# A quantised FFN on one Trainium2 core: new start-up transfers, down scales folded into the weights, two middle operations moved to GpSimd, deeper buffers

## The reference

```python
W = weights[condition]                       # (64, 32, 32), picked by token out of 16
y = einsum('bct,bcd->bdt', x, W)             # x: (64, 32, 512) f32
x_flat = y.reshape(-1, 512).astype(bfloat16) # 2048 rows
def _dynamic_quant(x, inv_smooth):
    xs = x.astype(float32) * inv_smooth
    scale = maximum(max(abs(xs), axis=-1) / 127, 1e-08)
    return clip(round(xs / scale), -127, 127), scale
gate_out = (qg @ w_gate.T) * sg * s_wgate    # 512 -> 256
up_out   = (qu @ w_up.T) * su * s_wup        # 512 -> 256
inter = clip(silu(gate_out) * up_out, -10, 10).astype(bfloat16)
qi, si = _dynamic_quant(inter, inv_inter)
out = x + (qi @ w_down.T) * si * s_wdown     # 256 -> 512
```

## Time and profile before

| | us |
|---|---|
| median of 3 runs | 96.28 |
| lowest and highest run | 96.28, 98.17 |
| span of the profiled execution | 96.0 |
| DVE busy | 72.1 (75%) |
| POOL busy | 67.5 (70%) |
| ACT busy | 62.9 (66%) |
| PE busy | 57.0 (59%) |

### The profile page before, as it was taken

How to read it: one execution, slowest core, us unless ns; L and a number is a source line. 1 busy time by engine, 2 the same in 40 slices (tenths; PEclk the granted TensorE clock), 3 DMA queues, 4 the chain that set the end, 5 groups by cost and what they waited for, 6 DMA issues and landing times.

```text
span 96.0 us, 1583 instructions
## 1 busy us (share of the span) xinstructions
PE 57.0 (59%) x425; PEld 36.1 (38%) x430; DVE 72.1 (75%) x174; ACT 62.9 (66%) x113; POOL 67.5 (70%) x57
## 2 busy tenths in 40 slices
PE   0692737189559487595865958569594574305610
PEld 0691214164426344363443635436352353102100
DVE  5300059407798989999999999999999999996360
ACT  5000226813978999889898898988989878223100
POOL 5505094800858759999999999999999746925720
PEclk9999999966999999999999999999999999965555
DMA  1989639989412312063360633202202022020443
GB/s 33 230 291 376 180 106 272 251 153 321 136 43 73 111 22 92 38 181 117 112 219 6 213 111 111 109 7 109 91 18 109 3 109 106 7 109 0 180 149 114
DMA packets 8796, 12.05 MB, mean 126 GB/s; under 512 B 3026, under 2 KB 3922, under 8 KB 8786
## 3 DMA queue, kind: packets, MB, share of 16 engines
q1 hardware_dynamic: 7906, 10.08, 33.0%
q0 software_dynamic: 400, 1.31, 3.8%
q10 hardware_dynamic: 480, 0.54, 2.7%
HBM read 7.47 MB, written 4.46 MB: 124 GB/s over the span
## 4 chain that ended last, share of the span: by engine, by line
DVE 54%; issue 13%; DMA 11%; PE 11%; ACT 4%; POOL 2%; SPq 1%; POOLq 0%; ACTq 0%
DVE y_ps L359 13%; DVE ffn L406 12%; DVE gu L373 10%; DVE gu_ps L378 7%; DMA raw<-in_L_ffn_w_down 6%; PE gu_ps L582 5%; DMA picked<-in_L_cond_weights,tokens 5%; DVE amax_m L390 4%; PE o_ps L610 3%; ACT q_t L269 3%; DVE rscale L367 2%; PE y_ps L560 2%; POOL raw L195 1%; DVE rest L414 1%; DVE rest_sums L418 1%
## 5 line engine op out<-in xcount | busy, mean ns | idle before, releaser
L206 POOL TENSOR_TENSOR xs<-y_bf,inv_in 128x1024 f32<-128x1024 bf16 x15 | 32.1, 2142 | 10.2 <-ACT y_bf L255 9.6
L582 PE MATMUL gu_ps<-w_t,q_t 128*128 128x256 bf16 x128 | 17.6, 283 | 17.4 <-ACT q_t L269 17.4
L262 ACT ACTIVATE q<-xs,rscale 128x512 f32<-128x512 f32 x32 | 21.4, 724 | 2.1 <-DVE rscale L367 2.1
L222 POOL TENSOR_TENSOR res<-ffn,x_sb 128x512 f32<-128x512 f32 x15 | 19.1, 1271 | 2.7 <-DVE ffn L406 2.7
L359 DVE TENSOR_REDUCE y_ps<-xs 128x2 f32<-128x1024 f32 x16 | 19.5, 1217 | 1.1 <-POOL xs L204 1.1
L560 PE MATMUL y_ps<-x_sb,mix_all 128*128 128x512 f32 x32 | 17.3, 625 | 4.7 <-DMA mix_all<-in_L_cond_weights 2.5
L582 PEld LDWEIGHTS gu_ps<-w_t,q_t 128*128 128x128 bf16 x128 | 11.7, 101 | 21.4 <-ACT q_t L269 20.0
L269 ACT ACTIVATE q_t<-qt_ps 128x1024 bf16<-128x1024 f16 x16 | 16.2, 1014 | 0.3 <-PE qt_ps L566 0.3
L255 ACT ACTIVATE y_bf<-y_ps 128x512 bf16<-128x512 f32 x16 | 9.3, 581 | 10.1 <-PE y_ps L560 10.1
L373 DVE TENSOR_TENSOR gu<-gu_ps,s_in 128x512 f32<-128x512 f32 x16 | 10.9, 683 | 5.5 <-PE gu_ps L582 5.5
L215 POOL TENSOR_TENSOR xm<-clipped,inv_mid 128x256 f32<-128x256 bf16 x16 | 11.7, 732 | 3.6 <-DVE clipped L385 3.6
(11 more groups left out here) (40 smaller groups left out, 54.1 us busy)
## 6 DMA issues: line engine op xcount, KB each, us to landing
x_sb<-in_x SPq DMA_DIRECT2D x16, 256.0 KB, 3.5
out<-res SPq DMA_DIRECT2D x16, 256.0 KB, 2.0
raw<-in_L_ffn_w_gate POOLq DMA_DIRECT2D x1, 512.0 KB
raw<-in_L_ffn_w_up POOLq DMA_DIRECT2D x1, 512.0 KB, 7.6
raw<-in_L_ffn_w_down SPq DMA_DIRECT2D x1, 512.0 KB, 5.6
inv_in<-in_L_ffn_inv_gate ACTq DMA_DIRECT2D x1, 256.0 KB, 4.2
inv_in<-in_L_ffn_inv_up ACTq DMA_DIRECT2D x1, 256.0 KB, 5.5
picked_dram<-picked SPq DMA_DIRECT2D x1, 256.0 KB, 3.2
```

The lines of the kernel that those rows point to most:

```text
L206: nc.gpsimd.tensor_tensor(xs[t % 2][:, :, :], y_bf[t % 2][:, :].unsqueeze(1).to_broadcast([P, 2, T]), inv_in[:, :, :], ALU.mult).then_inc( ...
L222: nc.gpsimd.tensor_tensor(res[t % RES][:, :], ffn[t % 2][:, :], x_sb[:, t * T:(t + 1) * T], ALU.add).then_inc(res_done, 1)
L262: nc.scalar.activation(q[t % 2][:, m, :], xs[t % 2][:, m, :], ACT.Copy, bias=ROUND_TO_F16, scale=rscale[:, t, m:m + 1]).then_inc(q_done, 1)
L582: last = nc.tensor.matmul(gu_ps[p][:, m, :], q_t[p][:, m, c, :], w_t[j][:, m, c * I:(c + 1) * I], start=(j == 0 and c == 0), stop=(j == pa ...
```

## The change

The host now lays the weights out: gate, up and down come already transposed by 128-row chunks, and all six vectors come as one row `vectors`. On the chip:

- **Vectors.** One transfer puts the row on one partition; five PE products with a row of ones (`widen`) spread it over 128 partitions in PSUM, and ACT and DVE copy the parts out. The broadcast transfers go.
- **Weights.** Gate and up products read the top halves of the f32 numbers directly as moving operand (every second bf16); the transposes and copies go. ACT issues their transfers, behind its first copy.
- **Down weights.** DVE multiplies w_down by s_down (`fold_s_down`) and splits the f32 result into three bf16 parts (`next_part`). Each down tile takes six products instead of two. `down_out` multiplies by the row scale and adds x, straight into `res`; POOL's `residual` goes.
- **Register loads.** The tokens for the early blocks are loaded from DRAM, in groups of two or four ahead of the transfers; the SBUF row goes.
- **Middle.** The clip and the middle quantisation are POOL's. The intermediate goes to SBUF as bf16. The scales of tile t+3 and of the middle of tile t are one operation over three columns, from SBUF to SBUF.
- **Buffers.** `xs` four, `y_bf`, `q`, `q_t`, `gu` and the middle's three each; the mix product waits for `ybf_done` and runs five tiles ahead.
- **End tiles.** Tiles 0 and 15 go through smoothing, maximum, quantisation and transposing in halves; tile 15's down product and output are two halves.
- 36 warming products instead of 52. The check of the weights' low bits moves to the start, and covers gate and up only.

```diff
-    WARM_UP = 52
+    WARM_UP = 36
...
+    XS, YB, QB, GB, MB = 4, 3, 3, 3, 3
+    MID_LAG = 3
...
@@ SP
-            sp.dma_start(token_row[:, :], token.unsqueeze(0)).then_inc(row_in, 16)
+            sp.dma_start(rows[:, :], vectors.unsqueeze(0)).then_inc(rows_in, 16)
             load(0)
-            load(1)
-            sp.wait_ge(row_in, 16)
...
+            for t in range(EARLY):
+                s = [sp.value_load(token.unsqueeze(0)[0:1, t * PER + j:t * PER + j + 1], min_val=0, max_val=S - 1)
+                     for j in range(PER if t == 2 else PER // 2)]
+                if t == 0:
+                    sp.wait_ge(mix_zero, 1)
+                for j in range(len(s)):
+                    early_block(t, j, s[j])
+                if t + 1 < EARLY:
+                    load(t + 1)
+            sp.dma_start(flat(raw_down), w_down).then_inc(w_down_in, 16)
+            load(3)
             sp.wait_ge(picked_in, 16)
             sp.dma_start(picked_dram, picked[:, :]).then_inc(picked_out, 16)
...
+            load(4)
             sp.wait_ge(picked_out, 16)
...
@@ POOL
+            def clip(t):
+                pool.wait_ge(inter_done, t + 1)
+                nc.gpsimd.tensor_scalar(clipped[t % MB][:, :], inter[t % MB][:, :], LIMIT, -LIMIT,
+                                        ALU.min, ALU.max).then_inc(clip_done, 1)
...
+            def quantise_mid(t):
+                pool.wait_ge(rscale_done, scales_through(t + MID_LAG, 2))
+                if t >= MB:
+                    pool.wait_ge(qmt_done, t - MB + 1)
+                nc.gpsimd.tensor_scalar(qm[t % MB][:, :], xm[t % MB][:, :], rscale[:, t + MID_LAG, 2:3], ROUND_TO_F16,
+                                        ALU.mult, ALU.add).then_inc(qm_done, 1)
...
+            for t in range(4):
+                smooth(t)
+            for i in range(TILES):
+                clip(i)
+                smooth_mid(i)
+                if exists(i + 4):
+                    smooth(i + 4)
+                quantise_mid(i)
...
@@ ACT
+            inv_gate_copy()
+            act.dma_start(raw[0][:, 0, :], w_gate).then_inc(w_in, 16)
+            act.dma_start(raw[0][:, 1, :], w_up).then_inc(w_in, 16)
+            y_out(0)
+            s_in_copy()
+            y_out(1)
+            y_out(2)
+            quantise(0)
+            y_out(3)
+            q_out(0)
+            quantise(1)
+            y_out(4)
+            for i in range(TILES + 1):
                 if exists(i):
+                    gate_silu(i)
+                if exists(i + 1):
+                    q_out(i + 1)
+                if exists(i + 2):
+                    quantise(i + 2)
+                if exists(i - 1):
+                    qm_out(i - 1)
+                if exists(i + 5):
+                    y_out(i + 5)
...
@@ DVE
+            rest_in_gate_up()
+            fold_s_down()
+            for i in range(TILES + 1):
                 if exists(i):
+                    gate_up_out(i)
+                if exists(i - 1):
+                    amax_mid(i - 1)
+                if i == LAST - 3:
+                    smooth_gate(LAST)
+                if i == LAST - 2:
+                    amax_half(LAST, 1)
+                scales(i + 2)
                 if exists(i):
+                    intermediate(i)
+                if i + 3 < LAST:
+                    amax_in(i + 3)
...
+                if i == 0:
                     raise_flag()
+                    next_part(1)
+                if i == 1:
+                    next_part(2)
+                if exists(i - 2) and i - 2 < LAST:
+                    down_out(i - 2)
+            for h in range(2):
+                down_out_half(h)
...
+                nc.vector.scalar_tensor_tensor(res[t % RES][:, :], o_ps[:, :], scale[:, t + MID_LAG, 2:3],
+                                               x_sb[:, t * T:(t + 1) * T], ALU.mult, ALU.add).then_inc(res_done, 1)
...
@@ PE
+            def widen(dst, at, n):
+
+                return nc.tensor.matmul(dst, ones_row[:, :], rows[:, at:at + n], start=True, stop=True)
...
+                        last = nc.tensor.matmul(gu_ps[p][:, m, :], q_t[a][:, m, c, :],
+                                                bf16_top(raw[j][:, m, c * I:(c + 1) * I]),
+                                                start=(j == 0 and c == 0), stop=(j == parts - 1 and c == TC - 1))
...
+            def down_products(a, dst, first, end):
+                for j in range(PARTS):
                     for c in range(IC):
+                        last = nc.tensor.matmul(dst, qm_t[a][:, c, :],
+                                                bf16_top(w_out[j][:, c, first:end]),
+                                                start=(j == 0 and c == 0), stop=(j == PARTS - 1 and c == IC - 1))
...
+            for t in range(4):
+                mix_in_batch(t)
             transpose_q(0)
+            mix_in_batch(4)
+            for i in range(TILES + 2):
+                if exists(i - 2):
+                    transpose_mid(i - 2)
                 if exists(i):
+                    gate_up(i)
...
+                if exists(i + 1):
+                    transpose_q(i + 1)
                 if exists(i - 2):
+                    down(i - 2)
+                if exists(i + 5):
+                    mix_in_batch(i + 5)
```

More of the change, by code:

```diff
@@ L14, with adaln_ffn @@
 ROUND_TO_F16 = float(3 * 2 ** 22 + OFFSET_BITS)
-def adaln_ffn(nc, x, token, mix_w, w_gate, s_gate, w_up, s_up, w_down, s_down, inv_gate, inv_up, inv_inter, out):
+def adaln_ffn(nc, x, token, mix_w, w_gate, w_up, w_down, vectors, out):
     B, C, T = x.shape
     S = mix_w.shape[0]
-    I = w_gate.shape[0]
     PER = P // C
     TILES = B * C // P
+    LAST = TILES - 1
     PARTS = 3
-    TC, IC = T // P, I // P
+    TC = T // P
+    I = w_gate.shape[1] // TC
+    IC = I // P
     EARLY = 3
-    WARM_UP = 52
+    WARM_UP = 36
     RES = 4
-    AHEAD = 4
+    XS, YB, QB, GB, MB = 4, 3, 3, 3, 3
+    MID_LAG = 3
+    AT_INV, AT_S_IN, AT_MID, AT_OUT = 0, 2 * T, 2 * T + 2 * I, 2 * T + 3 * I
     x_rows = x.rearrange("b c t -> (b c) t")
@@ L175, in _ @@
                              ).then_inc(blocks_in, 16)
-            sp.dma_start(inv_mid[:, :], inv_inter.partition_broadcast(P)).then_inc(mid_in, 16)
-            sp.dma_start(s_out[:, :], s_down.partition_broadcast(P)).then_inc(s_out_in, 16)
-            for t in range(4, 11):
+            for t in range(5, 12):
                 load(t)
-            for t in range(TILES):
+            for t in range(LAST):
                 store(t)
-                if exists(t + 11):
-                    load(t + 11)
+                if exists(t + 12):
+                    load(t + 12)
@@ new lines, in q_out @@
+                if split(t):
+                    for m in range(2):
+                        act.wait_ge(qt_done, 2 * t + 1 + m)
+                        nc.scalar.activation(q_t[t % QB][:, m, :, :], qt_half(t, m), ACT.Copy,
+                                             bias=-float(OFFSET)).then_inc(qt_out, 1)
+                else:
+                    act.wait_ge(qt_done, 2 * t + 2)
+                    nc.scalar.activation(q_t[t % QB][:, :, :, :], qt_ps[t % 2][:, :, :, :], ACT.Copy,
+                                         bias=-float(OFFSET)).then_inc(qt_out, 1)
@@ L420, in raise_flag @@
             def raise_flag():
                 dve.wait_ge(rest_total, 1)
[L422 removed]
+                nc.vector.tensor_copy(flag[:, :], flag_ps).then_inc(flag_done, 1)
             def again(t):
@@ L671, with by_chunks @@
     from concourse.bass_utils import run_bass_kernel_spmd
+    def by_chunks(w):
+        columns, contracted = w.shape
+        return np.ascontiguousarray(w.T.reshape(contracted // P, P, columns).transpose(1, 0, 2).reshape(P, -1))
+    laid_out = {
+        "x": inputs["x"], "token": inputs["itok_B_0_15"], "mix_w": inputs["L0_cond_weights"],
+        "w_gate": by_chunks(inputs["L0_ffn_w_gate"]), "w_up": by_chunks(inputs["L0_ffn_w_up"]),
+        "w_down": by_chunks(inputs["L0_ffn_w_down"]),
+        "vectors": np.concatenate([inputs[n] for n in (
+            "L0_ffn_inv_gate", "L0_ffn_inv_up", "L0_ffn_s_wgate", "L0_ffn_s_wup", "L0_ffn_inv_inter", "L0_ffn_s_wdown")]),
+    }
     nc = bacc.Bacc("TRN2", target_bir_lowering=False, num_devices=1)
     arrays, args = {}, []
-    for name in _INS:
-        a = np.ascontiguousarray(inputs[name])
+    for name, value in laid_out.items():
+        a = np.ascontiguousarray(value)
         arrays[f"in_{name}"] = a
```

563 lines of the change are left out of this document (251 added, 312 removed).

## The result

| | before | after |
|---|---|---|
| median, us | 97.22 | 112.66 |
| lowest and highest, us | 96.28, 99.25 | 112.32, 112.86 |
| span of the profiled execution, us | 96.0 | 110.8 |
| ratio after / before | | 1.1657, 95% interval 1.1593 to 1.172 |

The ratio and its interval go by the fast runs of both kernels alone, so the ratio isn't the quotient of the medians; in experiment 1 they leave out one run of 126.85 us.

A forecast was written before the change was run, and what follows sets the result against it. DVE and POOL together bound the middle, a chain of transfers the head. The terms 20.6 + 5.2 + 8.4 + 38.0 + 9.85 + 11.25 gave a 93.3 us span, with 0.28 added 93.6 us, range 89.5 to 99.0.

The forecast's parts named there:

- L: Head, SP's queue: time to load one register value from DRAM, 0.4 us taken; gather's store starts at 10.4 + 8L.
- Rival C: Head: eight DRAM register loads in series hold SP's queue; at L = 1.3 the time is 100.8 us; chance 17%.
- Landing of the store: Head: the store of the gathered blocks takes 2.8 us to land, against 3.26 in the kernel before.
- From the blocks to the first result: Head: from the landing of the fourth tile's blocks to the first gate/up result, 5.2 us at the low clock.
- The merged scale: Steady turn, DVE: the scale operation over three columns takes 0.15 us.
- rival D: Steady turn: the three-column scale is blocked by POOL's 2.11 us smooth; turn 4.2, time 98 us; chance 10%.
- The turn without the wait: Steady turn, PE and POOL setting the pace: 3.8 us, bounds 3.65 and 4.15; ten turns 38.0.
- Rival E: PE's products: strided moving operands run at half rate; turn 6.0, time 115 us; chance 3%.
- First two turns: DVE's first two turns, with later parts of w_down and the flag: 4.4 and 4.05, together 8.4 us.
- Last three turns: Turns without mix or whole smooth, last tile in halves: 3.65, 3.3 and 2.9, together 9.85 us.
- The tail: From the last gate/up result to the end of the span: 11.25 us, 2.7 of it twelve 256-column products.
- Around the span: Added to the 93.3 us span to get the median of the runs: 0.28 us, giving 93.6.

The follow-up runs named there:

- experiment 1: Changed kernel with its register loads read from SBUF again, after one small transfer of the token row: 101.81 us, ratio to the kernel before 1.0459.
- run 3: Changed kernel with two early tiles instead of three, so SP loads four registers from DRAM instead of eight: 108.12 us in one run.
- experiment 2: Changed kernel with the merged three-column scale cut into three one-column operations: 107.92 us, ratio to the kernel before 1.1149.
- experiment 10: Changed kernel with 52 warming products instead of 36: 112.96 us in one run.
- run 6: Changed kernel with both register loads from SBUF and one-column scale operations: 97.6 us, ratio to the kernel before 1.0055.
- run 4: Kernel before with the input maximum in SBUF instead of PSUM, so its two-column scale goes from SBUF to SBUF: 119.07 us in one run.
- experiment 5: Kernel before with the register loads of its early blocks read from DRAM, nothing else changed: 111.69 us in one run.
- number 8: Kernel of experiment 7 with the check of the low bits moved ahead of the first tile's smoothing: 95.53 us, ratio to the kernel before 0.9845.
- experiment 7: Changed kernel with SBUF register loads, one-column scales and a reordered head (four early blocks, earlier gather store, 52 warming products): 95.99 us, ratio to before 0.9865.

## Why the prediction was wrong, point by point

- **The register load, the step that failed worst.** The sum had L = 0.4 for one load. It argued from one end, "the nearest row is the same instruction by far", and that row read SBUF. What was mis-sized is not the latency alone: a value from DRAM is two loads in series, of which the trace of before could show neither. L, the two loads together, measured 1.60 in the mean, and 10.4 + 8L = 23.2 against 23.59 measured: the rest of that term held. That is 10.0 us of the head's 13.1. Rival C named the place and the mechanism; its L of 1.3 was still too low. "Issued in groups, several may be in flight" was the reason given against it, and no two loads overlap in the trace. The Trainium skill (Runtime: NRT & Kernel Launch, The launch sequence) tells of about 1.3 us for register loads from HBM; measured are 0.92 and 0.46 in the median for the pair, 1.39 together, so this figure was near. The Trainium skill (DMA: Bandwidth & Descriptors, Latency and other measured facts) has a floor of about 600 ns; the single load of 463 ns lies below it, the pair far above, and the measurement decides.
- **Landing of the store.** Forecast 2.8, measured 5.1 in the changed kernel and 7.2 in run 3: +2.3 us. The reason given, that less is in flight, didn't hold: the core moved 256 GB/s in that stretch of the changed kernel and 216 in the kernel before. That traffic is the cause isn't shown: experiments 2 and 10, with the changed kernel's order of transfers, have 4.3 and 4.4 us at 300 GB/s. From the scatters to mix(3) 4.2 was forecast, 4.0 measured.
- **From the blocks to the first result.** 5.2 forecast, 6.3 measured; the low clock was foreseen from the earlier trace rows, but lasted into the gate/up products as well (1.64 for 1.07). In run 6 the same stretch took 5.7.
- **The merged scale.** The forecast's price of 0.15 was wrong; rival D, given 10%, was right: it works the turn out as 4.2, and 4.17 is measured, with each of its parts within 0.1 us of the trace. The reason against it, that a scale of one column took 136 ns, was true, and carried over to three columns where it doesn't hold: 152 ns for one, 746 for three. Runs 2 and 4 show this both ways. The Trainium skill (VectorE: DVE Perf Modes, Mode 2×_2P) says that an operation with one SBUF source and an SBUF destination can read its tensor through both ports, split along its outermost dimension; with what the Trainium skill (SBUF — State Buffer, Who interferes with whom) says of the lock, this fits every scale operation here: two and three columns stand, one column and the two columns from PSUM don't. No run shows the ports themselves, and the reciprocal of three columns from SBUF to SBUF, 0.18 beside a smooth in run 2, shows that size and place of the operands don't settle it.
- **C and D as exclusive cases.** Both were listed with the time that each would give alone, and no case held both. They are independent, both occurred, and their prices add. The case of both, with C's L of 1.3, would have read 100.8 + 10 x 0.4 = about 105; even that is under 112.66, by the further 0.3 of L (2.4), the landing and the steps below.
- **The turn without the wait.** 3.8 forecast, PE and POOL setting it, 3.81 measured in run 2, with PE busy for 20.00 of the 20 us from 60 on and POOL for 19.16. Its parts: clip 0.40 and quantisation 0.48 on POOL (0.48 each forecast), smooth 2.15, smooth_mid 0.67. The moving operand of every second bf16 costs nothing: eight products take 1.07 us against 1.05 in the earlier trace rows. Rival E falls.
- **First two turns.** +0.8: a part of w_down (L481, both inputs in SBUF) and the smooth behind it stand in each other's way. In the changed kernel's timeline:

```profile
41.72 1.29 DVE L481 TENSOR_TENSOR w_out<-w_out 128x1024 f32<-128x1024 f32 x1
41.90 3.12 POOL L232 TENSOR_TENSOR xs<-y_bf,inv_in 128x1024 f32<-128x1024 bf16 x1
```

The smooth takes 3.12 instead of 2.15. The earlier trace rows had shown just that, and the sum priced the DVE operation alone. The first turn was even shorter than its forecast (4.04 for 4.4), the second took 5.14 for 4.05; with scales of one column it still took 4.78.
- **Last three turns.** 9.85 forecast, 11.1 to 11.2 in every version, even without both causes. "No wait closes a longer loop" fails here. PE's order puts transposes of the middle ahead of the next gate/up, and the middle's quantisation waits for a scale that stands behind the last tile's maximum. The pieces of the chain that ended last, changed kernel (start us, us, what):

```profile
97.79 0.69 DVE gu L443
98.48 0.34 DVE amax L455
98.84 0.17 DVE scale L425
99.03 0.17 DVE rscale L428
...
99.29 0.49 POOL qm L253
99.83 0.29 PE qmt_ps L646 x2
100.12 0.92 PE gu_ps L627 x8
101.06 0.69 DVE gu L443
```

From one gate/up result to the next, 3.27 us of pure latency that no engine's busy time shows; with the last tile's half maximum (0.59) and a second scale and reciprocal in it the turn before has 4.02. I had worked these turns out from DVE's load alone.
- **The tail.** 11.25 forecast, 9.74 measured. From the start of the last gate/up product it is 110.8 - 99.95 = 10.85 us, where it was 15.2: the one stretch of the sum that came out better than forecast. The last twelve products took 0.85 and 0.69 of the path, 1.54, where the sum had 2.7 (in proportion, two of 512 columns in 1.01 us even give 3.0); the granted clock is 1.00 from 106.5 to 108.1 us, where the old tail had 0.50 from 90 us on. So 1.2 of the 1.5 us by which the tail beat its forecast go with a higher clock that the forecast hadn't counted on: luck, not working.
- **Around the span.** 0.28 us was added; the changed kernel's profiled execution has 1.8. It is no part of the change: every later run of the kernel before on record lies 1.7 to 2.0 above its own span, and experiments 4 and 5 have 1.9. So the 0.28, the difference between a median of runs and the span of one execution, was no measure of this step, and the term was 1.5 us too small.
- **The widening products.** They ended at 14.4, not near 10 (in experiment 2 at 11.2), and were hidden all the same: experiment 10 ended them at 12.9 and gained nothing.

So the place of the loss is shown: two edits take back 15.1 of 15.4 us. The change's own gains are real. By the rows of the table, experiment 6 against the kernel before, the ten turns give 2.1 us, the last three 0.9 and the tail 3.6, together 6.6. The head and the first two turns take nearly all of it back, 5.0 and 1.2: the first gate/up result is taken at 27.2, where it was at 22.2. In PE's order the whole pipeline now waits for the fourth tile's blocks, whose mix product starts at 21.48. The best version run, number 8, is 1.5% below the kernel before (0.8 to 2.3%).

## What to carry to other kernels

Price an instruction by what it reads and where, not by its name: a register value from DRAM was two serial loads of 1.6 us together, one from SBUF 0.27. Beside a smooth a scale of three columns took 0.75 us where three of one column took 0.28 together, and a scale of two columns took 1.90 us from SBUF and 0.15 from PSUM. Merging small VectorE operations, or moving their input from PSUM to SBUF, can therefore be a loss when a GpSimd operation runs beside them, as both were here. List, for each VectorE operation, whether it has two SBUF inputs or is a scale of several columns from SBUF to SBUF, and what GpSimd does then. And where rivals can hold together, give their joint case a time and a chance of its own.

## What the runs showed of the hardware that I had not expected

- A register value from DRAM costs a load of its pointer (0.83 to 1.8 us, mean 1.13) and one of the value (0.46), not overlapped even where four are asked for in a row. The first value of experiment 5 took 2.6 and 2.0 us.
- A SBUF-to-SBUF scale stands behind a running GpSimd operation with two columns (1.90 us) and with three (0.75 in the mean, as it started later in the smooth), but not with one (0.13 to 0.15), and a reciprocal of three columns doesn't stand (0.18). The block works both ways: a VectorE operation with two SBUF inputs took 2.90 us for 1.23 behind a smooth, and a smooth behind such an operation 3.12 for 2.15.
- Widening products of 512 f32 columns ran at 1.9 us each from 6.4 to 14.4 us, as did mix(0) and mix(1) (1.84 each, 1.02 later), in a stretch whose granted clock the records give as 1.00. In experiments 2, 6 and 10 the first two took half of that each, with 36 or 52 warming products ahead of them; in experiment 2, with PE busy all the while, the granted clock then went from 1.00 to 0.50 between 8 and 9.3 us, and the products behind took 1.91 again. So 1.9 us goes with a recorded clock of 0.50 there and of 1.00 in the changed kernel; why is open.
- The same store of 256 KB landed after 3.1 to 7.2 us. It isn't shown what decides: experiments 7 and 8, with the same order of transfers, have 3.1 and 5.0 us, and the longest (experiment 3) had 283 GB/s beside it, less than the 322 beside the 4.0 us of experiment 1.
